# A sixteen-image transformer tower on one core: the last expert stage with its residual turned in two blocks, its last two token tiles cut into column halves, and ScalarE's closing steps in another order

## The reference

```python
def _L3_ffn_ref(x, W1, b1, Wg, bg, Wd, bd):      # 576 tokens, 64 -> 256 -> 8 experts of 64
    H = jax.nn.gelu(xf @ W1 + b1, approximate=False)
    probs = jax.nn.softmax((H @ Wg + bg) / TEMP, axis=-1)
    assign = jnp.argmax(probs, axis=-1)
    for e in range(Wd.shape[0]):
        y = H @ Wd[e] + bd[e]
        out = out + jnp.where((assign == e)[:, None], probs[:, e:e + 1] * y, 0.0)
    return out
h = _layernorm(h + _L3_ffn_ref(h, ...), axis=-1)  # and h is returned
```

## Time and profile before

| | |
|---|---|
| median of 3 runs | 167.77 us (166.68 to 168.07) |
| the profiled execution, its own time | 167.7 us |
| its span, first to last instruction | 165.8 us |
| granted TensorE clock, mean of the span | 0.993 |
| busy: PE, PEld, DVE, ACT, POOL | 88%, 43%, 62%, 43%, 19% |
| the stage that the diff touches, from L774 to the end | 146.3 to 165.8 us |

### The profile page before, as it was taken

The page is one execution under the profiler, slowest core; times in us unless marked ns, Lnnn a source line. Parts: engine busy times, 40 slices in busy tenths (PEclk is TensorE's granted clock), DMA queues, the critical chain, the costliest instruction groups (busy, mean ns, idle before and its releaser), DMA issues.

```text
span 165.8 us, 2878 instructions
## 1 busy us (share of the span) xinstructions
PE 145.2 (88%) x1109; PEld 71.7 (43%) x1122; DVE 102.8 (62%) x284; ACT 71.6 (43%) x133; POOL 32.1 (19%) x83
## 2 busy tenths in 40 slices
PE   6999889999999796979997995799879997999960
PEld 1455356544444352435552312266435554564420
DVE  7315777754558649387496899922858467113981
ACT  3726951766362000573530000616664065466423
POOL 7400000057779200001000001600049000000000
PEclk9999999999999999999999999999999999999997
DMA  5999970000000000000031000000000000000001
GB/s 170 329 425 328 259 298 0 4 2 0 2 6 0 0 0 0 4 0 0 0 57 54 0 0 2 0 4 0 0 0 4 0 0 4 0 0 4 2 0 36
DMA packets 4916, 8.26 MB, mean 50 GB/s; under 512 B 2747, under 2 KB 2875, under 8 KB 4774
## 3 DMA queue, kind: packets, MB, share of 16 engines
q1 hardware_dynamic: 4902, 8.07, 15.2%
HBM read 7.70 MB, written 0.37 MB: 49 GB/s over the span
## 4 chain that ended last, share of the span: by engine, by line
PE 59%; DVE 24%; ACT 7%; DMA 6%; issue 3%; DVEq 0%; ACTq 0%
PE ps L445 9%; PE ps L386 7%; PE ps L432 6%; DVE scores L1287 5%; PE ps L800 5%; PE ps L439 4%; PE ps L393 3%; PE ps L400 3%; DMA k_scratch<-k_parts_tok 2%; DVE scores_rest L1306 2%; DMA weights_sb<-weights 2%; PE ps L543 2%; PE ps L551 2%; DMA k_parts_img<-k_scratch 2%; DVE top L1294 1%
## 5 line engine op out<-in xcount | busy, mean ns | idle before, releaser
L386 PE MATMUL ps<-idle_operand 128*128 128x512 bf16 x140 | 39.1, 391 | 7.1 <-DVE scores L1287 1.7
L1097 DVE TENSOR_TENSOR hidden_gated<-hidden,ps 128x576 f32<-128x576 f32 x28 | 19.7, 751 | 10.1 <-PE ps L439 10.0
L862 ACT ACTIVATE hidden<-ps,weights_sb 128x576 f32<-128x576 f32 x28 | 19.4, 738 | 11.7 <-PE ps L432 9.2
L386 PEld LDWEIGHTS ps<-idle_operand 128*128 128x128 bf16 x153 | 13.0, 102 | 22.7 <-issue 4.1
L854 ACT ACT_TABLE_LOAD x16 | 20.5, 1283 | 0.3
L842 ACT ACTIVATE squares<-ps 128x288 f32<-128x288 f32 x8 | 3.3, 411 | 32.9 <-PE ps L445 9.0
L445 PE MATMUL ps<-hidden_gated,weights_sb 128*64 128x288 f32 x112 | 16.3, 418 | 0.0
L1036 DVE COPY centred<-ps 128x288 f32<-128x288 f32 x8 | 3.7, 457 | 17.3 <-ACT squares L842 17.3
L432 PE MATMUL ps<-h,weights_sb 64*128 64x288 f32 x80 | 13.1, 436 | 0.8 <-ACT hidden L862 0.6
L300 POOL CAST combine_parts_T<-combine_parts_T 48x288 f32<-48x288 bf16 x3 | 1.3, 418 | 63.3 <-DVE combine_parts_T L1068 63.3
L1287 DVE TENSOR_REDUCE scores<-ps 128x32 f32<-128x512 f32 (+1 forms) x15 | 8.8, 667 | 2.2 <-PE ps L686 2.2
(11 more groups left out here) (284 smaller groups left out, 230.4 us busy)
## 6 DMA issues: line engine op xcount, KB each, us to landing
patch_sb<-patches SPq DMA_DIRECT2D x6, 288.0 KB, 5.7
weights_sb<-weights SPq DMA_DIRECT2D x1, 1108.0 KB, 10.4
weights_sb<-weights SPq DMA_DIRECT2D x1, 717.0 KB, 14.7
weights_sb<-weights SPq DMA_DIRECT2D x1, 689.0 KB, 13.4
weights_sb<-weights SPq DMA_DIRECT2D x1, 640.0 KB, 7.8
weights_sb<-weights SPq DMA_DIRECT2D x1, 512.0 KB, 12.9
weights_sb<-weights SPq DMA_DIRECT2D x1, 394.0 KB, 13.5
weights_sb<-weights SPq DMA_DIRECT2D x1, 375.5 KB, 6.9
```

Source lines behind the costliest of these rows:

```text
L386: mm(PS[:, bank, :], idle_in[:, 0:P], idle_in[:, :], start=True, stop=True)
L862: act.activation(HR[:, at % RING, :, :], two(ZA if ch % 2 == 0 else ZB), func, bias=w(f"b1_{n}")[:, ch:ch + 1]).then_inc(S["act_out"], 1)
L1097: dve.tensor_tensor(HG[:, at % GRING, :, :], HR[:, at % RING, :, :], two(GATE_AT[n][ch]), ALU.mult)\
```

## The change

1. The residual of tiles 1 to 4 is turned with two matmuls in place of four: a block of `HP` is loaded once and all 128 identity columns are streamed, which gives both halves. ACT's copy L981 reads the result with another pattern, of the same 256 columns.
2. Tiles 3 and 4 are computed in two pieces of 256 columns (32 features each), each with its own bias, its two products and its own `y3_done`. The second pieces go to banks 5 and 7. DVE gates and sums each piece by itself; only the second one's sum reports the tile.
3. ACT's closing order becomes: squares 0, 1, 2; root; square 3; root; outputs 0, 1, 2; output 3; square 4; root. DVE's reciprocals for tiles 0 to 2 move ahead of tile 4, that of tile 3 stands in the middle of its second piece, and a third one is for tile 4 alone.

```diff
+        def pieces3(q):
+            return ((0, D // 2), (D // 2, D)) if q >= FT - 2 else ((0, D),)
+
+        def y3(q, a, b):
+            bank = (4, 0, 1, 2, 3)[q] if a == 0 else {FT - 2: G + 1, FT - 1: MB}[q]
+            return PS[0:64 if q == 0 else P, bank, 0:(b - a) * E]
...
-            for q in range(1, FT):
-                last = mm(PS[:, YB, q * D:(q + 1) * D], HP[:, ((q - 1) % 2) * P:((q - 1) % 2 + 1) * P],
-                          c("ident")[:, rows((q - 1) // 2)], start=True, stop=True)
+            for b in range(2):
+                last = mm(PS[:, YB, D + b * P:D + (b + 1) * P], HP[:, b * P:(b + 1) * P], c("ident"),
+                          start=True, stop=True)
...
             for q in range(1, FT):
-                bias(q)
-                part(q, 0)
-                part(q, 1).then_inc(S["y3_done"], 1)
+                for a, b in pieces3(q):
+                    if q == FT - 2 and a > 0:
+                        pe.wait_ge(S["exp_in"], 4)
+                    bias(q, a, b)
+                    part(q, 0, a, b)
+                    part(q, 1, a, b).then_inc(S["y3_done"], 1)
...
-            act.activation(YM[:, 1:FT, :, E], PS[:, YB, D:FT * D].rearrange("p (q d) -> p q d", d=D), ACT.Copy)\
+            act.activation(YM[:, 1:FT, :, E].rearrange("p (h b) d -> p h b d", b=2),
+                           PS[:, YB, D:D + 2 * P].rearrange("p (b h d) -> p h b d", b=2, h=2), ACT.Copy)\
...
             root3(0, 3)
+            squares3(3)
+            root3(3, 4)
             act.wait_ge(S["rs"], 9)
             for q in range(3):
                 out3(q)
-            squares3(3)
-            squares3(4)
-            root3(3, FT)
             act.wait_ge(S["rs"], 10)
             out3(3)
+            squares3(4)
+            root3(4, FT)
...
+                ins = dve.tensor_reduce(R[0:p, q, a:b], YM[0:p, q, a:b, :], AX, ALU.add)
+                if b == D:
+                    ins.then_inc(S["tile3"], 1)
+                else:
+                    step(ins)
...
+            done = 0
             for q in range(FT):
-                gated3(q)
                 if q == FT - 1:
                     rstd3(0, 0, 3)
-                summed3(q)
-            rstd3(1, 3, FT)
-            dve.wait_ge(S["rs"], 10)
+                for a, b in pieces3(q):
+                    done += 1
+                    dve.wait_ge(S["y3_done"], done)
+                    gated3(q, a, b)
+                    if q == FT - 1 and b == D:
+                        rstd3(1, 3, 4)
+                    summed3(q, a, b)
+            rstd3(2, 4, FT)
+            dve.wait_ge(S["rs"], 11)
```

More of the change, by code:

```diff
@@ L782, in tok3 @@
                 return HH[:, ch, 4 * P:TOK] if q == 0 else HH[:, ch, (q - 1) * P:q * P]
-            def y3(q):
-                return PS[0:n3(q), 4 if q == 0 else q - 1, :]
             for h in range(2):
                 mm(PS[32 * h:32 * h + 32, YB, 0:D], HP[:, 2 * P:HALF], c("ident")[:, rows(h)], start=True, stop=True)
-            for q in range(1, FT):
-                last = mm(PS[:, YB, q * D:(q + 1) * D], HP[:, ((q - 1) % 2) * P:((q - 1) % 2 + 1) * P],
-                          c("ident")[:, rows((q - 1) // 2)], start=True, stop=True)
+            for b in range(2):
+                last = mm(PS[:, YB, D + b * P:D + (b + 1) * P], HP[:, b * P:(b + 1) * P], c("ident"),
+                          start=True, stop=True)
             last.then_inc(S["hres"], 1)
@@ L794, in _, with bias, part @@
             wd = w("Wd").rearrange("p (c f) -> p c f", c=2)
[L796 to L800, removed]
+            def bias(q, a=0, b=D):
+                mm(y3(q, a, b), one3[:, 0:n3(q)], BD3[:, a * E:b * E], start=True, stop=False, skip_group_check=True)
+            def part(q, ch, a=0, b=D):
+                return mm(y3(q, a, b), tok3(q, ch), wd[:, ch, a * E:b * E], start=False, stop=(ch == 1),
+                          skip_group_check=True)
             def logits_T(ch):
@@ L1370, in rows3, with gated3, summed3 @@
                 return 64 if q == 0 else P
-            def gated3(q):
+            def gated3(q, a, b):
                 p = rows3(q)
[L1374 to L1379, removed]
+                step(dve.tensor_tensor(YM[0:p, q, a:b, 0:E],
+                                       y3(q, a, b).rearrange("p (d e) -> p d e", e=E),
+                                       comb[0:p, q, :].unsqueeze(1).to_broadcast([p, b - a, E]), ALU.mult))
+            def summed3(q, a, b):
                 p = rows3(q)
@@ L1382, in summed3 @@
                 sync()
-                dve.tensor_reduce(R[0:p, q, :], YM[0:p, q, :, :], AX, ALU.add).then_inc(S["tile3"], 1)
+                ins = dve.tensor_reduce(R[0:p, q, a:b], YM[0:p, q, a:b, :], AX, ALU.add)
[3 more added lines that the diff above has]
+                    step(ins)
             def rstd3(n, a, b):
```

## The result

The changed kernel takes 166.25 us (median of 6 runs, 165.53 to 166.60) against 167.48 us (median of 6, 166.68 to 168.07) for the kernel before in the same comparison. The ratio is 0.9924, with a 95% interval of 0.9898 to 0.9949: 1.3 us less, between 0.9 and 1.7. The forecast was 166.9, a gain of 0.9 that would not stand clear of the scatter of 1%, and the range of 166.0 to 167.9 holds the time.

The account below looks back on a forecast made before the run. Output 0's release of SP and output 3's existence were taken to bind together. Residual, pieces and closing order moved the last issue 0.88 us: 167.7 - 0.9 = 166.8, plus 0.07 for the median, 166.9; range 166.0 to 167.9.

Parts of the forecast that it names:

- What bounds: At the closing stores, output 0 letting SP start and output 3 existing bind together; afterwards SP's issuing, output 4 0.2 earlier.
- Part 1: Residual's turn on PE: four fewer records at 0.13 each save 0.47 us, passed on to everything behind.
- the hand-over: On PE, from the residual to the bias behind it: 0.04 us left out of the 0.51 that goes.
- Part 2 on PE: Tiles 3 and 4 in pieces: added loads fit under halved records of 0.215, so a split tile stays at 1.94 us.
- B: Rival on PE: added weight loads are exposed, a split tile takes 2.80 us, total 167.8, no change; chance 0.09.
- C: Rival on PE: halved records cost nearly a whole one each, at the bound 3.88 a tile and 169.9 us; chance 0.03.
- Part 2 on DVE: Tiles 3 and 4: a piece takes 0.90 us, a split tile 1.80 instead of 1.45, so DVE becomes the pace.
- what it wins: DVE's gain from pieces: PE's last piece no longer has a whole gate and sum behind it.
- Part 3: Closing order on ACT, DVE and SP: output 0 starts 160.38, output 4 is written by 162.77, last issue 163.00.
- The sum: SP's last store issue moves from 163.88 to 163.00, -0.88 us, giving 166.9 us.
- A: Rival at the residual: its 0.47 us does not pass on, gain 0.41, total 167.4; chance 0.20.
- D: Rival at SP's stores: spacing stays 0.39, output 4 binds, last issue moves -1.09, total 166.7; chance 0.06.

Follow-up runs that it names:

- Experiment 9: Changed kernel with tile 1's store cut into two of half the columns, seven issues instead of six: stage time 17.11 us against 16.64; run once, no ratio.
- 10: Changed kernel with tile 0's two stores issued by POOL, leaving SP four: stage time 16.46 us against 16.64; run once, no ratio.
- experiment 1: Kernel before with only the residual's turn in two products and the copy's new pattern: stage time 17.19 us against 17.58, ratio 0.9975.
- 11: Changed kernel with the old residual in four products and the copy's old pattern: stage time 17.03 us against 16.64; run once, no ratio.
- Experiments 4: Changed kernel with tiles 3 and 4 whole, all else kept: stage time 16.58 us against 16.64; ratio 0.9944 to the kernel before.
- 2: Kernel before with only ACT's new closing order and DVE's three reciprocals placed as in the change: stage time 16.98 us against 17.58, ratio 0.9982.
- the second one: Second timed comparison, the changed kernel again without an edit against the kernel before: ratio 0.9934 (0.9913 to 0.9955), median 166.44 us, stage time 16.63.
- experiment 3: Kernel before with only the column halves of tiles 3 and 4, ACT's old order, old residual: stage time 17.27 us against 17.58, ratio 0.9963.

## Why the prediction was right, point by point

**What bounds.** Right. The prediction said that SP's start by output 0 and the existence of output 3 bind together, and that after the change SP's own issuing is last, with output 4 some 0.2 ahead. Experiment 9 (one issue more, 0.47) and 10 (two fewer, 0.18 back and then output 4) show both.

**Part 1.** The mechanism was right, the size was off: 0.47 forecast, 0.39 measured, in the trace of the changed kernel and in experiments 1 and 11. The mis-sized term is the price of four records: 0.52, and 0.04 for the hand-over, where the chain now has 0.64. The prediction divided the time of a whole group by its count, 1.03 / 8 and 1.31 / 10, and took the quotient of 0.13 for the price of a record. But a group's time has a fixed part, and the fewer the records, the more of it each one carries. The answers for each line, two of the kernel before and one of the kernel after, min/median/max in ns:

```profile
L701 PE MATMUL ps<-consts_sb,probs x10: 272/272/328, 108.2 to 109.3; 128*128 128x128 f32 x10
L790 PE MATMUL ps<-consts_sb,h x8: 275/275/323, 147.7 to 148.5; 128*128 128x64 f32 x8
```

```profile
L796 PE MATMUL ps<-consts_sb,h x4: 275/275/377, 147.1 to 147.5; 128*128 128x128 f32 x4
```

The longest record of each group is its first, and the last one shows its whole length. What is left is the pace from one record to the next, and it is the same in all three: L701 (1.31 - 0.27 - 0.06) / 9 = 0.11, L790 (1.10 - 0.275 - 0.05) / 7 = 0.11, L796 (0.71 - 0.275 - 0.10) / 3 = 0.11. So four records at 0.11 went, 0.44, and the longer first record gave 0.05 back. Why that record is 0.10 longer in L796 and 0.06 in L701, which has the same shape, no run shows.

**Part 2 on PE.** Right: 0.98 a piece where 0.97 was forecast. The rival of exposed loads (B) needed 1.40 a piece, and C up to 1.94; both are out. The Trainium skill's sentence ("TensorE: Matmul & The Clock Gate", "The mechanism") that weight loads overlap matmuls in flight only where the row group differs does not hold in this stage: eight loads of 191 ns, all on the same rows, were added and each tile took 0.02 longer. The start of the same section also allows the overlap when the load goes to a background weight buffer, and that fits; no run here tests it.

**Part 2 on DVE.** Right: gates of 0.41 (forecast 0.42), sums of 0.45, a piece in 0.89 (0.90), DVE the pace of tiles 3 and 4. But the text let one sum stand for three parts and did not ask what the halves are worth alone. Its own numbers held the answer: it has tile 3's sum end at 159.64, and before it ended at 160.06, from this row:

```profile
159.30 0.76 DVE L1383 TENSOR_REDUCE residual<-patch_sb 128x64 f32<-128x576 f32 x1
```

That is 0.42 earlier, of which 0.47 was the residual's. So 0.05 is a loss by the halves on the way to output 0. Experiments 4 against the changed kernel and 2 against 11 measured 0.06 and 0.05 of stage time, a loss, in this order of the end. The loss also shows that "what it wins", the shorter end behind PE's last piece, was not on the path that binds.

**Part 3.** Right in each link. In stage time, output 0 was forecast at 14.08 and came at 14.02, output 4 written at 16.47 and 16.43, the last issue at 16.70 and 16.64. The 0.08 that the residual fell short was made up on ACT: tile 3's sum ended 0.06 later than forecast (13.40 for 13.34), and from the root's start to output 0 it was 0.20 for 0.32, as the prediction had left out the overlap of these two. The reciprocal between tiles 3 and 4 saved 0.04 more (158.99 to 159.07, 0.08 for 0.12), on the way to output 4 alone.

**The sum.** 0.88 forecast, 0.94 measured on the stage. By parts the prediction's numbers imply 0.47 for the residual, some 0.46 for the order and -0.05 for the halves; measured were 0.39, 0.60 and -0.06. That the shortfall of the first and the surplus of the second nearly cancel is luck. The 166.9 also rests on a median of 167.77 before; in the comparison that median was 167.48, 0.29 less. The timed comparison says 1.3 and its interval begins at 0.9; the second one says 0.0066 of 167.43, 1.1 us, with 0.7 to 1.5 as its interval. The 0.94 lies inside both intervals. Nothing in the traces of the stage answers to what the timed runs show above it; whether there is more is not known.

**The rivals.** A (the residual does not pass) is out by experiment 1. D rested on a spacing of 0.39, seen behind the gap in the earlier trace rows. Without a gap SP keeps 0.47; 0.39 comes after an issue that had to wait, and so again in experiment 3 (163.25 to 163.63).

## What to carry to other kernels

When a kernel ends in a row of stores from one queue, the last byte is late by the number of issues times their spacing after the *first* output, so an early output is worth as much as the last one; count both, and expect the smaller slack to be all that a reordering yields. Cutting the last tiles does not help when the engine that takes them over then has more to do than it gained by starting earlier: compare the two (0.27 against 0.32 for tile 3, 0.35 against 0.30 for tile 4), and do it at the tile that the binding output waits for. And price each part of a change by itself even when they go in together, because a sum that comes out right can hide a part that costs.

## What the runs showed of the hardware that was not expected

- On SP the issue of one of these stores is spaced 0.47 from the next, at 32 KB, at 16 KB (experiment 9) and at 8 KB (tile 0, 160.42 to 160.89) alike; an issue that had waited for its output is shorter (0.33 to 0.36, against 0.43) and the next follows after 0.37 to 0.40. The first issue of each kernel is such a one.
- POOL's two stores in experiment 10 (8 KB each) took 1.27 us to issue and 1.9 to land (median), where SP's two took 1.4 in the changed kernel; from the last issue to the execution's end it was 3.72, against 3.79 in the changed kernel, so the slower queue cost nothing with early outputs.
- Two groups with the same shape in the grouped rows can differ in their weight loads: 0.140 for the transposes of L701, 0.191 for the products with the identity of L790, both 128 x 128 f32. The pace of their records is 0.11 all the same.
